# A gated attention kernel: global attention's division and output projection moved from the last stage into the first chunks of the local layers

## Time and profile before

| what | value |
|---|---|
| median of 3 runs | 2410.58 us (2409.3 to 2415.99) |
| the profiled execution | 2411.07 us, of which its span is 2409.0 us |
| busy share of the span | TensorE 93%, VectorE 70%, ScalarE 57%, GpSimd 25% |
| local layers, g = 0 and 1 | about 887 to 1010 us of the span |
| local layers, the rest | to about 2338.5 us |
| combine | from about 2338.7 us to the end |

### The profile page before, as it was taken

One profiled execution on the slowest core, in us unless ns is written; L12 is line 12 of the kernel. 1 busy time (PEld: TensorE's weight loads), 2 busy tenths in 40 slices (PEclk: granted clock), 3 DMA queues, 4 the chain that ended last, 5 costly groups with the idle time before them and its releaser, 6 DMA issues. The chain is left out here.

```text
span 2409.0 us, 40563 instructions
## 1 busy us (share of the span) xinstructions
PE 2239.6 (93%) x12576; PEld 1301.2 (54%) x12576; DVE 1685.6 (70%) x3777; ACT 1362.6 (57%) x2570; POOL 594.6 (25%) x482
## 2 busy tenths in 40 slices
PE   7969999999999978899999999899999999999968
PEld 4534333333333336666666666566566667666534
DVE  5778999999999936676576666666666666657326
ACT  2216777777777765565465555455556546546321
POOL 4411200000000015432333233233233334233000
PEclk9968999999999998999999999999999999999989
DMA  4584112211211010000000000000100000000016
GB/s 147 190 248 131 56 44 62 62 48 50 62 53 57 28 51 1 1 1 1 0 0 0 0 0 0 27 1 9 35 1 1 0 0 0 0 0 0 0 32 192
DMA packets 71891, 95.83 MB, mean 40 GB/s; under 512 B 13884, under 2 KB 49168, under 8 KB 71696
## 3 DMA queue, kind: packets, MB, share of 16 engines
q1 hardware_dynamic: 71808, 94.78, 12.9%
HBM read 60.67 MB, written 39.49 MB: 42 GB/s over the span
## 5 line engine op out<-in xcount | busy, mean ns | idle before, releaser
L655 DVE TENSOR_REDUCE maxima<-ps_m 128x1 f32<-128x512 f32 x1024 | 635.2, 684 | 63.0 <-PE ps_m L546 59.0
L718 ACT ACTIVATE probs<-ps_st 128x1024 f32<-128x1024 f32 x512 | 496.2, 1021 | 172.4 <-PE ps_st L578 170.9
L546 PE MATMUL ps_m<-k_st,q_st 48*128 48x512 f32 x1024 | 391.3, 469 | 31.8 <-DMA k_st<-ks 15.7
L1259 ACT ACTIVATE l_probs<-l_probs,l_neg_max 128x256 f32<-128x256 f32 x512 | 254.1, 497 | 217.3 <-DVE l_neg_max L1395 217.3
L578 PE MATMUL ps_st<-q_st,k_st 50*128 50x512 f32 x1024 | 307.3, 427 | 1.6 <-ACT probs L718 0.6
L578 PEld LDWEIGHTS ps_st<-q_st,k_st 50*128 50x128 f32 x1024 | 161.0, 187 | 222.7 <-ACT probs L718 192.2
L591 PE MATMUL ps_o<-probs,v_st 128*32 128x512 f32 x2048 | 274.5, 608 | 0.6 <-ACT probs L718 0.6
L1395 DVE CUSTOM_DVE_ANT_1 l_probs<-ring,l_mask 128x256 f32<-128x256 f32 x384 | 140.1, 421 | 178.7 <-PE ring L1073 178.2
L546 PEld LDWEIGHTS ps_m<-k_st,q_st 48*128 48x128 f32 x1024 | 172.2, 190 | 147.8 <-DVE maxima L655 125.3
L1238 ACT COPY p_turned<-ring 128x512 f32<-128x512 f32 x256 | 139.7, 595 | 160.4 <-PE ring L1033 160.3
L992 POOL TENSOR_SCALAR clipped<-sumsq 128x16 f32<-128x16 f32 x64 | 16.1, 252 | 764.3 <-DVE sumsq L1372 764.3
(11 more groups left out here) (150 smaller groups left out, 3840.1 us busy)
## 6 DMA issues: line engine op xcount, KB each, us to landing
qs<-split SPq DMA_DIRECT2D x16, 512.0 KB, 3.5
ks<-split SPq DMA_DIRECT2D x16, 512.0 KB, 5.1
q_st<-qs SPq DMA_DIRECT2D x64, 128.0 KB, 2.6
k_st<-ks SPq DMA_DIRECT2D x64, 128.0 KB, 3.2
o<-o_sb SPq DMA_DIRECT2D x32, 256.0 KB, 2.3
x_in<-in_L_attn_x_dram SPq DMA_DIRECT2D x8, 512.0 KB, 6.1
v<-v_sb SPq DMA_DIRECT2D x16, 256.0 KB, 4.7
q_st<-qs SPq DMA_DIRECT2D x64, 64.0 KB, 2.9
```

The costliest lines, as they stand in the source:

```text
L546: nc.tensor.matmul(bank(base, use)[:, :], q_st[u][r, qt * P:(qt + 1) * P], k_st[u][r, h * CH:(h + 1) * CH], start=True, stop=True).then_in ...
L655: nc.vector.tensor_reduce(maxima[:, par, side(e), tile + e // 4, e % 2:e % 2 + 1], bank(base, k + e)[:, :], AX_X, ALU.max).then_inc(m_used, 1)
L718: nc.scalar.activation(probs[:, kt % 4, j, :], ps_st[j][:, :], ACT.Exp, scale=float(G_DIM) ** -0.5).then_inc(exp_done, 1)
L1259: nc.scalar.activation(probs[:, head, :], probs[:, head, :], ACT.Exp, bias=neg_max[:, head:head + 1], scale=-1.0, accum_out=total[:, head: ...
```

## The change

- `combine` no longer loads sums and products, inverts, spreads, divides or projects. It computes silu, multiplies with the projected attention, transposes, adds x and stores. The multiplication of one half of the channels goes to GpSimd. Its loops are written out.
- The division and the projection are done in g = 0 and g = 1 of the local layers, one chunk in each window from W = 1 on, and the last one (chunk 7) behind W = 7. The sums of all chunks are inverted at once, written to DRAM (`inv_dram`), and loaded back repeated over the 16 channels of a head. The projected chunk is copied out of PSUM by ScalarE (`take_s`) and stored to DRAM (`s_dram`).
- At the end of the local layers SP loads six projected chunks into the place of `wqkv` and six chunks of x into the place of the position tables and `rope_a`, `rope_b`, as soon as these are free. The last two of each are loaded in `combine`.
- SP's wait for the last `o_stored` moves from the end of `global_attention` into `local_layers`, behind the loads of the tables.

```diff
@@ global_attention, sync
                 body(ITERS - 1, False, True)
-                for c in range(2):
-                    sp.wait_ge(o_stored[c], UNITS // 2 * 16)
@@ local_layers
+        o_raw, o_inv, o_n, w_out, s_sb = hidden[:, 0:KD, :], hidden[:, KD:2 * KD, :], mid[:, :, 1:], dev, gate
+        sums, inv_sums = hidden[:, 0, :], hidden[:, 2 * KD, :]
@@ local_layers, tensor
+                def project_o(c):
+                    if c == 0:
+                        pe.wait_ge(w_out_in, 16)
+                    pe.wait_ge(divided, c + 1)
+                    for m in range(KD):
+                        if c:
+                            pe.wait_ge(s_copied, KD * (c - 1) + m + 1)
+                        for f in range(KD):
+                            mm = nc.tensor.matmul(ffn[m][:, :], w_out[:, f * D + m * P:f * D + (m + 1) * P], o_n[:, f, :], start=(f == 0), stop=(f == KD - 1))
+                        mm.then_inc(s_ready, 1)
                 def body(g, la, lf, before_hidden=None):
...
+                        if forward and w == 0 and isinstance(g, int) and g == 2:
+                            pe.wait_ge(s_copied, KD * CHUNKS)
                         if new:
                             project(g, w, (0, 1))
...
                         if mid_:
                             scores(W, w, 0)
+                        if not forward and W:
+                            project_o(W - 1)
...
                         if mid_:
                             scores(W, w, 1)
+                        if not forward and W == CHUNKS - 1:
+                            project_o(W)
@@ local_layers, sync, behind load_tables(1)
+                sp.dma_start(w_out[:, :].rearrange("p (k n) -> p k n", k=KD), w_out_t.rearrange("(k p) n -> p k n", p=P)).then_inc(w_out_in, 16)
+                for c in range(2):
+                    sp.wait_ge(o_stored[c], UNITS // 2 * 16)
+                sp.dma_start(sums, o_dram.rearrange("u (s r) n -> (u s) r n", r=2 * G_DIM)[:, 0, :]).then_inc(sums_in, 16)
+                sp.wait_ge(inverted, 1)
+                sp.dma_start(inv_dram.rearrange("u s n -> (u s) n"), inv_sums).then_inc(inv_stored, 16)
+                sp.wait_ge(inv_stored, 16)
+                for c in range(CHUNKS):
+                    if c:
+                        sp.wait_ge(divided, c)
+                    for f in range(KD):
+                        src = o_dram.rearrange("(i u) (j h r) n -> i h (u j) r n", u=4, j=2, h=2)[2 * (c // 2) + f, c % 2]
+                        sp.dma_start(o_raw[:, f, :], src[:, 1:1 + G_DIM, :]).then_inc(o_in, 16)
+                        src = inv_dram.rearrange("(i u) (j h) n -> i h (u j) n", u=4, j=2)[2 * (c // 2) + f, c % 2]
+                        sp.dma_start(o_inv[:, f, :], src.unsqueeze(1).broadcast_to([8, G_DIM, CH])).then_inc(o_in, 16)
+                    if c:
+                        store_s(sp, c - 1)
+                store_s(sp, CHUNKS - 1)
...
+                sp.wait_ge(s_stored, 16 * CHUNKS)
+                sp.wait_ge(v_mm, WPC * LAST)
+                wt.load_s(sp, s_dram, s_stored)
+                sp.wait_ge(qk_ready, WPC * LAST)
+                wt.load_x(sp, x, x_early)
@@ local_layers, scalar
+                def take_s(c):
+                    if c:
+                        act.wait_ge(s_stored, 16 * c)
+                    for m in range(KD):
+                        act.wait_ge(s_ready, KD * c + m + 1)
+                        nc.scalar.copy(s_sb[:, m, :], ffn[m][:, :]).then_inc(s_copied, 1)
...
+                        if not forward and W:
+                            take_s(W - 1)
                         if mid_:
                             exponentials(W)
+                        if not forward and W == CHUNKS - 1:
+                            take_s(W)
@@ local_layers, vector
+                def divide(c):
+                    dve.wait_ge(o_in, 16 * 2 * KD * (c + 1))
+                    if c:
+                        dve.wait_ge(s_ready, KD * c)
+                    nc.vector.tensor_tensor(o_n, o_raw, o_inv, ALU.mult).then_inc(divided, 1)
+
+                def invert():
+                    dve.wait_ge(sums_in, 16)
+                    nc.vector.reciprocal(inv_sums, sums).then_inc(inverted, 1)
...
                         if new:
                             rotate(g, w, la)
+                        if not forward and W == 0:
+                            invert()
+                        if not forward and W:
+                            divide(W - 1)
                         if next_one and not forward:
                             take_next(g, la, lf)
...
                             normalise(W, 1)
+                        if not forward and W == CHUNKS - 1:
+                            divide(W)
@@ combine, after
+            def _(act):
+                for n in range(CHUNKS):
+                    for k in range(KD):
+                        if n >= 2:
+                            act.wait_ge(gated_done[k], n - 1)
+                        nc.scalar.activation(silu[:, n % 2, k, :], xnt[:, k, n, 1:], ACT.Silu).then_inc(silu_done[k], 1)
+            def _(pool):
+                for n in range(CHUNKS):
+                    arrived(pool, n)
+                    pool.wait_ge(silu_done[1], n + 1)
+                    if n >= 2:
+                        pool.wait_ge(turned_back, 2 * n - 2)
+                    nc.gpsimd.tensor_tensor(gated[:, n % 2, 1, :], attention(n, 1), silu[:, n % 2, 1, :], ALU.mult).then_inc(gated_done[1], 1)
...
+                gate(0)
+                for n in range(CHUNKS):
+                    if n + 1 < CHUNKS:
+                        gate(n + 1)
+                    add(n)
```

More of the change, by code:

```diff
@@ L380, in global_attention @@
         o_copied = sem("o_copied")
-        o_stored = [sem(f"o_stored{c}") for c in range(2)]
         HALF = 2 * TILES
@@ L771, in __init__ @@
         self.b2 = per("b2_l", [P, KD])
+        self.tables = per("tables", [P, TILES, 4, HDIM])
+        self.rope = [sb(f"rope_{n}", [P, 2, INNER]) for n in "ab"]
         self.mask = sb("l_mask", [P, 4, P])
@@ L857, in local_layers @@
         sem = lambda n: ctx.enter_context(nc.semaphore(n))
-        tables = [sb(f"tables{l}", [P, TILES, 4, HDIM]) for l in range(DEPTH)]
+        tables, (rope_a, rope_b) = wt.tables, wt.rope
+        h = [sb(f"h_{n}", [P, KD, CH], F32R) for n in ("high", "low")]
         scales = sb("scales", [P, DEPTH, 2, HDIM])
-        h = [sb(f"h_{n}", [P, KD, CH], F32R) for n in ("high", "low")]
         v_ring = sb("v_ring", [P, WPC, INNER])
@@ L1611, in _ @@
[L1611 to L1630 removed]
+                for n in range(EARLY, CHUNKS):
+                    sp.dma_start(s_late[:, n - EARLY, :, :], s_dram[n]).then_inc(s_late_in, 16)
@@ new lines, in _ @@
+                for n in range(EARLY, CHUNKS):
+                    src = x[n // 2, n % 2 * CH:(n % 2 + 1) * CH, :].rearrange("(t p) n -> p t n", p=P)
+                    sp.dma_start(x_late[:, n - EARLY, :, :], src).then_inc(x_late_in, 16)
+                for n in range(CHUNKS):
+                    sp.wait_ge(summed, 2 * n + 2)
+                    dst = out[n // 2, n % 2 * CH:(n % 2 + 1) * CH, :].rearrange("(t p) n -> p t n", p=P)
+                    sp.dma_start(dst, result[:, n % 2, :, :]).then_inc(out_stored[n % 2], 16)
@@ L1654, in invert @@
-                def invert(b):
-                    dve.wait_ge(sums_in, 16 * (b + 1))
-                    nc.vector.reciprocal(inv_sums[0:SUMS, bass.ds(b % 2, 1), :].rearrange("p o n -> p (o n)"), sums[:, :]).then_inc(inverted, 1)
-                def gate(b, c, first):
-                    dve.wait_ge(silu_done, 2 * b + c + 1)
-                    for m in range(KD):
-                        dve.wait_ge(s_ready, 4 * b + 2 * c + m + 1)
-                        nc.vector.tensor_tensor(gated[:, c, m, :], ps_s[m][:, :], silu[:, c, m, :], ALU.mult).then_inc(gated_done, 1)
@@ L1704, in project @@
[L1704 to L1716 removed]
+                for n in range(CHUNKS):
+                    for k in range(KD):
+                        pe.wait_ge(gated_done[k], n + 1)
+                    if n >= 2:
+                        pe.wait_ge(summed, 2 * n - 2)
```

214 lines of the change are left out of this document (75 added, 139 removed).

## The result

| | before | after |
|---|---|---|
| median, run side by side | 2410.64 us (4 runs, 2409.3 to 2415.99) | 2393.03 us (4 runs, 2390.95 to 2395.54) |
| ratio | | 0.9923, 95% interval 0.9905 to 0.9942 |
| profiled execution (span) | 2411.07 us (2409.0) | 2390.95 us (2388.5) |

The account below looks back on a forecast made before the run. TensorE was taken to bound most of the local layers, a chain of waits g = 0 and 1. -42.6 - 1.7 + 4.9 + 9.45 + 14.7 = -15.25 us gave 2395 us against 2410.58; range 2383 to 2411.

Parts of the forecast that it names:

- the likeliest case: Whole kernel: the forecast's own case, a time of 2388 to 2402 us, chance 0.57.
- a landing of 3.5 us: Combine: each result store was taken to land 3.5 us after issue, giving 4.9 us for two chunks.
- the forecast's own round: Combine: two additions (1.3), the store's issue (0.1) and its landing (3.5) make 4.9 us for two chunks.
- a repeated load like that of `k_st` (3.2): W = 1: the repeated load was taken to last 3.2 us, so that o_in is complete at 912.4.
- the third rival, late o_in: Late o_in at W = 1, `divide` held 3.8 us more, or slow landings at the end: 2402 to 2412 us, chance 0.20.
- the forecast's 4.9: W = 1: cost of the first chunk's division and projection, 4.9 us more, bounds 2.4 and 8.7.
- 2.35 us for each window: W = 2 to 6: copies ahead of the exponentials on ScalarE cost 2.35 us a window, counted for three windows.
- There I count 1.2: W = 2 and 4, projection at the low clock, ScalarE already waiting before: 1.2 us more for each.
- the chain that was forecast: W = 7: exponentials, `normalise`, `divide`, `project_o` and copy in a row before g = 2, 14.7 us more, bounds 11 and 18.5.
- The rival `project_o` at 1.2 GHz: Local layers: the projection runs at 1.2 GHz in all windows, 3.6 x 6 = 22 us more, 2417 us, chance 0.06.
- The held `divide`: Local layers: GpSimd holds `divide`, `project_o` starts 4.1 us later in each window, 30 us more, 2425 us, chance 0.05.
- The early loads: End of local layers: 6 MB of loads cost nothing, hidden by forward work; without that cover some 20 us in combine.

Follow-up runs that it names:

- the other execution of the same code before (18.01): Kernel before with only the wait for the last o stores moved into the local layers; 2413.3 us in a single run, W = 1 took 18.01 us.

## Why the prediction was right, and where not

- **The sign and the size.** 2395 was forecast, 2393.03 measured, inside the likeliest case. The makeup was right: a large gain in combine, most of it paid back in W = 1 to 7. That the total came within 2 us is in part luck: W = 1 cost 3.1 more than counted and W = 2 to 6 cost 3.3 less, which cancel; combine gave 2.0 more. Three parts that the forecast put at nothing gave 3.1 together in the two profiled executions (1.49, 0.48 and 1.11). They are not tied to the change. The last store of o is issued between 883.08 and 887.64 us in the fourteen traces, with the same code ahead of it. From `turn_probs` to the end of the local layers it took 1326.75 to 1329.36 us in the eleven kernels with early loads, 1329.02 and 1329.20 in the kernel before without and with the wait moved. And the 0.48 is there with only the wait moved too (22.49 us from the first local instruction to W = 1, against 23.14 before and 22.66 after).
- **Combine.** The step "a landing of 3.5 us" was mis-sized: 2.9 at the median, which by the forecast's own round (1.3 + 0.1 + 2.9) gives 2.15 us a chunk. Measured are 2.24 from the first addition (2368.10) to the last (2383.79), instead of 2.45. The forecast of GpSimd's product (1.2 us) was right (1264 ns where nothing held it), but that it would hold VectorE's product in this stage was not in the sum. The eight products took 7.8 us, where unheld ones at 0.68 would take 5.4. So VectorE, which the forecast had at 2.0 us a chunk, is nearly full in this stretch, and a faster landing alone would give at most the 1.55 us that it was idle there.
- **The moved wait**: 1.77 and 1.78 us in two kernels, forecast 1.7.
- **W = 1.** The step that failed is "a repeated load like that of `k_st` (3.2)". The load landed 6.47 us behind its issue. It repeats each row to 16 partitions and has 256 KB, those of `k_st` repeat each row to 2 and have 128 KB; which of this makes the difference no run shows. So the third rival, late o_in, held in part: `divide` came 5.28 us behind the start of the first scores and was held 0.5 us; in other executions it came up to 6.7 us behind and lasted up to 2.65 us. With two of the four loads out of the way the window costs 21.15 - 16.28 = 4.87 us. That this is the forecast's 4.9 confirms no term: the repeated load still took about 5.2 us, and two issues are gone. Against the other execution of the same code before (18.01) the prices are 6.25 and 3.1.
- **W = 2 to 6.** The mechanism was half right, and two sizes were off. The copies do stand ahead of the exponentials, and these end where the forecast had them (t + 8.1 in W = 6, forecast t + 8.2), but neither moving them nor bringing the second scores forward shortens the windows by more than 0.8 us. "2.35 us for each window" measured 1.8 to 2.3. "There I count 1.2", for the windows at a low clock, measured -0.13 and 0.26: there the clock, not ScalarE's waiting, took the work up, since it rose to 1.00. That term is 2.3 of the 3.3 us. TensorE has 15.3 to 15.7 us of work in windows of 15.8 to 16.7. For the length of a window this sum fits: TensorE's load at full clock (11.8) plus 3.6, plus a remainder of about 1. The forecast's table of stretches averaged this away: 91 of 119 us busy over W = 0 to 7, but 3.6 us more fills a window of 14.5 that has 2.7 us to spare.
- **The rival `project_o` at 1.2 GHz** is out: W = 2 to 6 run at 1.00. Only the projections behind the long pauses were slow, as the forecast had it (5.35 us in W = 1, 6.23 for chunk 7). Its reason, that the clock was low only behind longer pauses, doesn't fit the rows of before: the matmuls of q and k in W = 4 started every 0.43 us behind a pause of 1.79 us, and those in W = 3 every 0.23 us behind one of 1.76.
- **W = 7.** 14.85 against 14.7, by the chain that was forecast (exponentials to t + 8.1, `divide` to t + 10.7, an idle of 6.06 us, a slow projection). With `divide` off the chain 8.2 us of it go away: more than half of the price was that of the order, not of the work.
- **The held `divide`.** A window that lets it happen costs what was said (4.0 to 4.9 us, with a wait and a copy added), though by another sum. In the kernel after it occurs at W = 1 only; the other seven take 1.21 or 1.22 us. `take_next` at W = 7 was held as forecast (3.43 us for two instructions instead of 1.29), and the exponentials still ended at t + 8.1.
- **The early loads** cost nothing that the traces can show (the range above; the kernel without them took 1328.03 us from `turn_probs` to the end of the local layers), as said; without their cover combine is 17.6 us longer, forecast "some 20".

## What to carry to other kernels

Work moved from a stage at the end into an earlier one can be paid mostly at its edges: here W = 1, and W = 7 with the last chunk, cost 23 of 29 us, and the five windows between them 6. Before costing a window, add the new work to the busiest engine's load in that window alone, not to the stage's mean; the same goes for calling an engine "not full". Take single windows from more than one execution before explaining them. A moved step's last instance wants its inputs early, and a buffer that frees in time.

## What the runs showed of the hardware

- A load that repeats each row to 16 partitions, issued with three others, landed 6.47 us behind its issue, and about 5.2 us with one other like it beside it, where the 128 KB repeated loads of `k_st` took 3.2 at the median.
- GpSimd's wide operations and VectorE hold each other in both directions: `divide` 1.74 to 2.65 us instead of 1.22, the scaling 2.70 to 2.84 instead of 1.90, a copy of 128x128 with one input 2.36. GpSimd's power operation of 128x16 (2.93 us) held none of the divisions beside it.
- Filling TensorE's pauses raised its granted clock: without the projection three of the windows W = 1 to 6 ran at 0.81 to 0.90 in each of three traces, with it W = 2 to 6 ran at 1.00 in ten. A window at 0.89 took up 3.6 us of work and grew by 0.3 us.
- SP's issues of 512 KB loads took 0.35 to 0.53 us for the first eight, and 2.1 to 2.3 us for every second one of the rest, with the DMA engines busy 80% or more in each slice of that time.
